# Layer 0 of a graph network: the record columns of the edges loaded turn by turn on SyncE

## What is computed

```python
edge_w = edge_attr @ nn_w.T + nn_b
msg = jax.nn.relu(x[src] * edge_w)
out = x @ root + bias
for r in range(N_REL):
    mask = edge_type == r
    m = jnp.where(mask[:, None], msg, 0.0)
    s = jax.ops.segment_sum(m, dst, num_segments=n)
    cnt = jax.ops.segment_sum(mask.astype(x.dtype), dst, num_segments=n)
    mean = s / jnp.maximum(cnt, 1.0)[:, None]
    out = out + mean @ W[r]
```

## Time and profile before

| | us |
|---|---|
| median of 3 runs | 6186.73 |
| lowest and highest run | 6183.74, 6193.87 |
| span of the profiled execution, first to last instruction | 4913.3 |
| edge stage of layer 0 in that span | 813.1 to 1386.7 |

### The profile page before, as it was taken

The page is one execution under the profiler, slowest core; times in us unless marked ns, Lnnn a source line. Parts: engine busy times, 40 slices in busy tenths (PEclk is TensorE's granted clock), DMA queues, the critical chain, the costliest instruction groups (busy, mean ns, idle before and its releaser), DMA issues. The chain is left out here.

```text
span 4913.3 us, 109595 instructions
## 1 busy us (share of the span) xinstructions
PE 3943.9 (80%) x22466; PEld 3257.1 (66%) x22467; DVE 3417.9 (70%) x9239; ACT 1796.7 (37%) x5526; POOL 3122.8 (64%) x3449
## 2 busy tenths in 40 slices
PE   6799995888987889878898466785978788478886
PEld 3577774777876677767777355674856666267664
DVE  7788885667757778577786667866247778755665
ACT  0455552221123333333332100002247667257774
POOL 0266664777756777667776677766677773057775
PEclk9999997999998999989999677997979889677877
DMA  1233334845516455164551687742456445134444
GB/s 45 92 125 128 125 126 102 212 126 157 161 49 190 137 150 156 55 192 136 150 157 31 208 255 217 247 125 65 148 166 133 106 106 127 43 99 108 109 109 100
DMA packets 651843, 647.50 MB, mean 132 GB/s; under 512 B 316126, under 2 KB 557860, under 8 KB 651716
## 3 DMA queue, kind: packets, MB, share of 16 engines
q0 software_dynamic: 145968, 374.55, 27.2%
q1 hardware_dynamic: 407764, 217.31, 16.2%
q10 hardware_dynamic: 97984, 54.35, 3.6%
HBM read 468.18 MB, written 176.82 MB: 131 GB/s over the span
## 5 line engine op out<-in xcount | busy, mean ns | idle before, releaser
L973 POOL DMA_INDIRECT G<-h_dram,idx x1572 | 1519.8, 967 | 537.1 <-issue 353.7
L1148 PEld LDWEIGHTS ps_a<-hotm,msg 128*128 128x128 f32 x4716 | 689.1, 194 | 199.3 <-DVE arena L1237 65.9
L1136 PE MATMUL ps_e<-nnw,attT 128*128 128x256 f32 x2358 | 736.3, 396 | 100.4 <-DVE prodm L1230 46.6
L1148 PE MATMUL ps_a<-hotm,msg 128*128 128x128 f32 x4716 | 730.6, 283 | 92.4 <-DVE arena L1237 91.6
L1237 DVE TENSOR_TENSOR arena<-ps_a,arena 128x256 f32 x1404 | 588.1, 419 | 215.6 <-issue 102.2
L768 POOL DMA_INDIRECT rec_dram<-rec,pos x392 | 376.4, 960 | 424.2 <-ACT rec L631 362.7
L973 POOL DMA_INDIRECT G<-feat_dram,idx x420 | 405.0, 964 | 350.9 <-POOLq L242 223.3
L1183 ACT ACTIVATE msg<-prodm 128x256 f32<-128x256 f32 x786 | 327.5, 417 | 670.9 <-DVE prodm L1230 602.5
L790 POOL DMA_INDIRECT rec_dram<-now,to x396 | 383.4, 968 | 186.3 <-POOL to L787 103.6
L1714 POOL DMA_INDIRECT arena<-rel_dram,idx x393 | 383.8, 977 | 123.9 <-issue 86.2
L1136 PEld LDWEIGHTS ps_e<-nnw,attT 128*128 128x128 f32 x2358 | 368.0, 196 | 137.8 <-DVE prodm L1230 67.3
(11 more groups left out here) (354 smaller groups left out, 7906.1 us busy)
## 6 DMA issues: line engine op xcount, KB each, us to landing
gate<-rec_dram SPq DMA_DIRECT2D x126, 384.0 KB
G<-msg_dram SPq DMA_DIRECT2D x300, 128.0 KB
msg_dram<-msg ACTq DMA_DIRECT2D x270, 128.0 KB
rel_dram<-stage SPq DMA_DIRECT2D x25, 1040.0 KB
G<-h_dram,idx POOLq DMA_INDIRECT x1572
msg_dram<-arena ACTq DMA_DIRECT2D x90, 128.0 KB
at<-edge_attr SPq DMA_DIRECT2D x98, 112.0 KB
attT<-attT_dram SPq DMA_DIRECT2D x74, 144.0 KB
```

The costliest lines, as they stand in the source:

```text
L973: pool.indirect_dma_start(G[:, n % width, :], None, table, bass.IndirectOffsetOnAxis(ap=idx[:, which, n:n + 1], axis=0)).then_inc(sem(f"sw ...
L1136: t.matmul(ps_e[s % BANKS][:], attT[:, s // HU, s % HU, :], nnw[:], start=True, stop=True).then_inc(sem("ew"), 1)
L1148: last = t.matmul(ps_a[s % BANKS][:, h, :], of[:, h * P:(h + 1) * P], hot[:, s, :], start=True, stop=True)
```

## The change

The columns of a turn now come in two turns ahead of their use (AHEAD0 = 2), all on SyncE. SyncE's first transfer has the columns of turn 0 alone (18 chunks), and then come six transfers of attributes. Once the first has landed, the columns of turns 1 and 2 follow (36 chunks), and only then the weights W, root and bias. After that each half turn brings three transfers of attributes of three chunks each (edge_rows; before, one of nine) and one transfer of columns for the turn after next (columns_in, nine chunks or fewer), which waits until the transfer of columns before it has landed. ScalarE issues no loads.

VectorE lays out the indices: those of turn 0 between two halves of the memset, those of turns 1 and 2 in turn 0 at step 9, and from turn 1 on, at step 9 of each turn, those of the turn after next. GpSimd casts nothing, and waits at each turn for its indices. TensorE waits for attributes every 3 units instead of every 9. VectorE's walk has one seam more (at turn 9), and its last two turns are written out instead of looped. Layers 1 and 2 keep the order of their work.

```diff
-        FIRST = 3 * U
+        AHEAD0 = 2
-        def columns_of(pool, first, end, loaded, loads):
...
-                        att = sb(pctx, "att", [P, 2, HU, A32]) if l == 0 else None
+                        att = sb(pctx, "att", [P, U, A32]) if l == 0 else None
...
-                                    sp.dma_start(meta[:, 0:FIRST, :], meta_rows[:, 0:FIRST, :]).then_inc(sem("meta_in0"), 16)
...
+                                def columns_in(turn, half, late):
+
+                                    sp.wait_ge(sem("meta_in"), (turn * 2 - 4 + half) * 16)
+                                    if late:
+                                        lo, hi = ((0, HU), (HU, FRONT))[half]
+                                        sp.dma_start(late_meta[:, ds(turn - SEAM), lo:hi, :].rearrange("p t s w -> p (t s) w"),
+                                                     rec_d[ds((turn * FRONT + SEAM * BACK + lo) * P, (hi - lo) * P), WMETA:WMETA + NMETA].rearrange(
+                                                         "(j p) w -> p j w", p=P)).then_inc(sem("meta_in"), 16)
+                                    else:
+                                        first = turn * U + half * HU
+                                        sp.dma_start(meta[:, ds(first, HU), :],
+                                                     rec_d[ds(first * P, HU * P), WMETA:WMETA + NMETA].rearrange(
+                                                         "(j p) w -> p j w", p=P)).then_inc(sem("meta_in"), 16)
+
+                                def edge_rows(i, h, after, late):
+
+                                    for q in range(h * (HU // QU), (h + 1) * (HU // QU)):
+                                        count = min(FRONT - q * QU, QU) if late else QU
+                                        if count <= 0:
+                                            continue
+                                        first = (i * FRONT + SEAM * BACK if late else i * U) + q * QU
+                                        sp.wait_ge(sem("attT"), upto(first + count - 1 - FRONT if after else first + QU - 1 - U))
+                                        sp.dma_start(att[:, q * QU:q * QU + count, :], rec_d[ds(first * P, count * P), WA32:REC].rearrange(
+                                            "(j p) w -> p j w", p=P)).then_inc(sem(f"att_in{q}"), 16)
...
+                                    sp.dma_start(meta[:, 0:U, :], meta_rows[:, 0:U, :]).then_inc(sem("meta_in"), 16)
+                                    for h in range(2):
+                                        edge_rows(0, h, False, False)
+                                    sp.wait_ge(sem("meta_in"), 16)
+                                    sp.dma_start(meta[:, U:3 * U, :], meta_rows[:, U:3 * U, :]).then_inc(sem("meta_in"), 16)
+                                    weights()
                                     extra_meta(0)
                                     halves = KD // BACK // 2
                                     with nc.sync.Fori(1, 1 + halves) as i:
                                         for h in range(2):
-                                            edge_columns(i, h, False, False)
+                                            edge_rows(i, h, False, False)
+                                            columns_in(i + AHEAD0, h, False)
                                             extra_meta(i * 2 - 1 + h)
...
+                                    with nc.sync.Fori(SEAM - AHEAD0, SEAM) as i:
+                                        for h in range(2):
+                                            edge_rows(i, h, False, False)
+                                            columns_in(i + AHEAD0, h, True)
...
+                                    with nc.sync.Fori(SEAM + 1, TURNS1 - AHEAD0) as i:
+                                        for h in range(2):
+                                            edge_rows(i, h, True, True)
+                                            columns_in(i + AHEAD0, h, True)
+                                        extras(i)
+                                    with nc.sync.Fori(TURNS1 - AHEAD0, TURNS1) as i:
+                                        for h in range(2):
+                                            edge_rows(i, h, True, True)
+                                        extras(i)
...
-                                    columns_of(pool, 0, FIRST, "meta_in0", 1)
-                                    gather_rows(pool, (0, FIRST - HU), h_d, 0, G, "prod", units=True)
-                                    columns_of(pool, FIRST, NU, "meta_in1", 1 + KD // BACK)
-                                    gather_rows(pool, (FIRST - HU, NU), h_d, 0, G, "prod", units=True)
+                                    for k in range(TURNS1):
+
+                                        pool.wait_ge(sem("columns"), k + 1)
+                                        gather_rows(pool, (k * U, (k + 1) * U), h_d, 0, G, "prod", units=True)
...
-                                        if s % HU == 0:
-                                            pe.wait_ge(sem(f"att_in{s // HU}"), (i + 1) * 16)
+                                        if s % QU == 0:
+                                            pe.wait_ge(sem(f"att_in{s // QU}"), (i + 1) * 16)
...
-                                if l == 0:
-                                    nc.scalar.dma_start(meta[:, FIRST:SEAM * U, :], meta_rows[:, FIRST:SEAM * U, :]).then_inc(sem("meta_in1"), 16)
-                                    for q in range(KD // BACK):
-                                        first = SEAM * U + q * FRONT
-                                        nc.scalar.dma_start(late_meta[:, q, 0:FRONT, :], meta_rows[:, first:first + FRONT, :]).then_inc(sem("meta_in1"), 16)
...
-                                v.memset(arena[:], 0.0).then_inc(sem("zeroed"), 1)
-                                dve.wait_ge(sem("zeroed"), 1)
+                                if l == 0:
+                                    half = KD * D // 2
+                                    v.memset(arena[:, 0:half], 0.0).then_inc(sem("zeroed"), 1)
+                                    dve.wait_ge(sem("meta_in"), 16)
+                                    v.tensor_copy(idx[:, 0, 0:U], meta[:, 0:U, 1]).then_inc(sem("columns"), 1)
+                                    v.memset(arena[:, half:KD * D], 0.0).then_inc(sem("zeroed"), 1)
+                                    dve.wait_ge(sem("zeroed"), 2)
...
+                                for c0, c2, c8 in walk(nc.vector, TURNS1, 0, 2, 8, seams=(KEPT, SEAM - AHEAD0, SEAM) if l == 0 else (SEAM,), late=True,
+                                                       static=AHEAD0 if l == 0 else 0):
+                                    if c0 and c0[2] == HU and l == 0:
+                                        n, i, s = c0
+                                        if isinstance(i, int) and i == 0:
+
+                                            dve.wait_ge(sem("meta_in"), 32)
+                                            v.tensor_copy(idx[:, 0, U:3 * U], meta[:, U:3 * U, 1]).then_inc(sem("columns"), 2)
+                                        elif not (isinstance(i, int) and i + AHEAD0 >= TURNS1):
+
+                                            dve.wait_ge(sem("meta_in"), (i + AHEAD0 - 1) * 32)
+                                            to = idx[:, 0, ds(n - HU + AHEAD0 * U, FRONT if c0.phase >= 2 else U)]
+                                            of = (late_meta[:, ds(i + AHEAD0 - SEAM), 0:FRONT, 1].rearrange("p t s -> p (t s)") if c0.phase >= 2
+                                                  else meta[:, ds(n - HU + AHEAD0 * U, U), 1])
+                                            v.tensor_copy(to, of).then_inc(sem("columns"), 1)
...
-                                        if l == 0:
-                                            dve.wait_ge(sem("columns"), i + 1)
```

More of the change, by code:

```diff
@@ L974, in gather_rows @@
                     ap=idx[:, which, n:n + 1], axis=0)).then_inc(sem(f"sw_g{n % width}"), 16)
-        FIRST = 3 * U
+        AHEAD0 = 2
         meta_rows = rec_d[0:NC1 * P, WMETA:WMETA + NMETA].rearrange("(j p) w -> p j w", p=P)
-        def columns_of(pool, first, end, loaded, loads):
-            pool.wait_ge(sem(loaded), 16 * loads)
-            if first == 0:
-                last = nc.gpsimd.tensor_copy(idx[:, 0, first:end], meta[:, first:end, 1])
-            else:
-                nc.gpsimd.tensor_copy(idx[:, 0, first:SEAM * U], meta[:, first:SEAM * U, 1])
-                last = nc.gpsimd.tensor_copy(idx[:, 0, SEAM * U:NU].rearrange("p (t s) -> p t s", s=U)[:, :, 0:FRONT],
-                                             late_meta[:, :, 0:FRONT, 1])
-            last.then_inc(sem("columns"), (end - first) // U)
-            pool.wait_ge(sem("columns"), end // U)
         def gathered_by(passes, s):
@@ L1063, in edge_columns @@
                                     before = first + count - 1 - FRONT if after else first + HU - 1 - U
-                                    if l == 0:
```

(27 more changed lines are left out.)

30 lines of the change are left out of this document (19 added, 11 removed).

## The result

The changed kernel is **slower**: a median of 6196.32 us (14 runs, 6186.22 to 6211.70) against 6184.12 us (14 runs, 6174.08 to 6194.97) of the kernel before, a ratio of 1.0022 with a 95% interval of 1.0012 to 1.0031. The forecast was 6170, some 17 us faster, with a range that ended at 6186.

A forecast was written before the change was run, and what follows sets the result against it. GpSimd was taken to pace layer 0's edge stage up to the seam, then a VectorE–TensorE chain. Terms -22.4 + 1.0 + 3.7 + 1.0 = -16.7 us gave 6170.0 from 6186.73, range 6160 to 6186.

The forecast's parts named there:

- the lead of 22.4 us: Layer 0's edge stage: earlier first gather, vanished idle time and pauses of GpSimd together, claimed as the gain at the seam.
- The first gather, -7.0 us: Start of layer 0: GpSimd's first gather at about 826.0 instead of 833.08, after VectorE's cast between the memset's halves.
- the idle 14.08 us, -13.8: Start of layer 0: GpSimd's wait for a first free slot shrinks to the usual 0.30 us.
- the first columns land no sooner: Rival: first columns of layer 0 land at 832 instead of 819.5; gain only 9.7 us, time 6177; chance 0.13.
- What the memset does to gathers: Start of layer 0: the memset's second half beside the first gathers costs them nothing.
- so a shift of GpSimd's start lasts to the seam: Layer 0: GpSimd paces up to the seam, so its earlier start, worth 22.4 us there, lasts to the end.
- no pause of GpSimd over 2 us up to the seam: Layer 0 before the seam: a sign in the trace that would show the forecast right.
- The casts, +1.0 and +3.7: VectorE's casts in layer 0: +1.0 us in early turns by delaying gathers, +3.7 in thirteen late turns at 0.28 each.
- TensorE +1.0: Late turns of layer 0: three more waits for attributes per turn, 0 to 2.2 us, taken as +1.0.
- SyncE's queue: Layer 0: SyncE's 6 attribute and 2 column loads per turn fit in its time; taken as 0.
- the slower rival: Layer 0: SyncE's queue gets late, columns land late and VectorE stands at step 9; up to 6216 us; chance 0.10.
- what fills that is untouched: The 1273.4 us between the profiled span of 4913.3 and the median 6186.73 were taken as unaffected by the change.

The follow-up runs named there:

- e9: As e1, but ScalarE's 16 column loads at the start are back and SyncE's later column loads are left out; ratio 1.0014 to the kernel before.
- e0: The kernel before, run once more unchanged for a trace to lay beside the changed kernel's; 6185.23 us, span 6183.0.
- e1: Changed kernel with 48 already met waits (24 instructions) ahead of VectorE's later loop, which then lies in three pieces; ratio 0.9979 to the kernel before.
- e10: Changed kernel with 96 already met waits (48 instructions) ahead of VectorE's later loop, which lies in three pieces; ratio 0.9990 to the kernel before.
- e11: Changed kernel with 256 already met waits (128 instructions) ahead of VectorE's later loop, which lies in four pieces; ratio 1.0067 to the kernel before.
- e2: Kernel before with 180 already met waits (90 instructions) ahead of VectorE's later loop, which then lies in four pieces; ratio 1.0053 to the kernel before.
- e5: As e1, with every later load of columns made twice on SyncE, the second into a buffer nothing reads; ratio 0.9986 to the kernel before.

## Why the prediction was wrong

Two steps failed. The sign was wrong because of a term that the sum does not have at all: what the longer program of VectorE does to a loop behind layer 0. And the sum lets the lead of 22.4 us pass through layer 0 with a loss of 5.7, where the traces show it shrinking to 13.8 at the seam and 4.0 at turn 25. Point by point:

- **The first gather, -7.0 us, and the idle 14.08 us, -13.8**: right at the start, not at the seam. The first columns had landed in time, the cast began 10.2 us into the stage (12.3 forecast) as the memset started earlier than in the first trace, the first message came at +21.7 (+22 forecast), and the lead at turn 1 was 22.1 us against a sum of -22.4. But the prediction has the 22.4 as the gain at the seam, and there it was 13.8. The rival "the first columns land no sooner" did not come.
- **What the memset does to gathers**: right, they take 0.95 us beside its second half.
- **"so a shift of GpSimd's start lasts to the seam, where GpSimd paces, and from there to the end"**: that the start reaches the end holds by e9 (15 to 21 us lost when it is undone), the reason does not. In the timed executions GpSimd does not set the pace: from turn 2 to turn 24 of e0 it stands waiting for free slots for 211.6 us, and where VectorE waits ahead of a message and the profile names no releaser, the gather of its rows had been issued 22 us or more before:

```profile
POOL G L973 <- DVE msg L1226: 211.6, 119, 9.9
```

The chain between TensorE, ScalarE and VectorE sets it. TensorE's waits in the first trace, 912 to 1364 us:

```profile
PE ps_a L1148 <- DVE arena L1237: 38.6, 36, 2.3
PE ps_e L1136 <- DVE msg L1226: 8.0, 11, 1.0
```

and in e0, turns 2 to 24 (1027 to 1650 us):

```profile
PE ps_e L1136 <- ACT attT L1169: 86.8, 51, 4.6
PE ps_a L1148 <- DVE arena L1237: 42.0, 34, 3.0
PE ps_a L1148 <- issue: 20.6, 15, 2.2
PE ps_e L1136 <- issue: 13.1, 14, 2.4
```

The waits for ScalarE and those for nothing visible are new. The sign that the prediction names, no pause of GpSimd over 2 us up to the seam, fails with them, in e0 as in the changed kernel.

- **The casts, +1.0 and +3.7, TensorE +1.0**: together too small for what layer 0 lost. The price of a cast was too low, but the runs do not show that casts make up the difference. The view of the cast's line in the changed kernel:

```profile
L1250 DVE CAST idx<-meta x23: 166/227/306, 987.4 to 1611.5; - x19, 128x13 int32<-128x13 f32 x3, 128x18 int32<-128x18 f32 x1
L1250 DVEq FUSED_REGOPS  x19: 93/105/123, 987.0 to 1611.3; - x19
L1250 DVEq ALU_OP  x12: 45/45/45, 1322.8 to 1611.4; - x12
```

A cast with its two register instructions is 0.38 us, not 0.28, which makes 4.9 in 13 turns. Gathers were not held up: in the changed kernel the 21 that ran beside one of these casts took 0.94 to 0.95 us, so the +1.0 of the early turns is not seen. With the loop in three pieces the change gains 13 us (e1, 0.9979; the 6 of e10 include some 7 of its own waits), where the sum had 16.7 and its bounds 10.5 to 22.4. But the stage itself, up to its last sum, is shorter by only 3.1 us in the changed kernel than in e0, and by 0.5, 5.5 and 1.6 in e1, e10 and e11 than in e2 (e10 and e11 on another chip). Where the rest of the 13 us lies, single profiles do not show.
- **SyncE's queue, and the slower rival**: it did not come. VectorE waits for no columns at step 9, and doubling the column loads (e5) changed nothing that can be told from no change. This rival forecast the right sign, at a chance of 0.10, but for a reason that the traces rule out; that it was slower is no credit to it.
- **"what fills that is untouched"**: wrong, as is the sentence ahead of the prediction that it rests on. The 1273.4 us were not outside of the span; the trace showed an execution that took a fifth less time than any timed one (4913.3 against 6183.0). A trace whose span doesn't fit the time by a fifth should have been a warning that its pace is not the timed one's.
- **The term that failed**: the sum has no line for what the change does to stages behind layer 0. It has no term for the new seam and the two written-out turns of VectorE, and gives no reason why they should be nothing. They and the casts are 373 instructions of code, and they moved a later loop over a boundary: some 27 us, which turned some 13 us gained (e1) into 12 lost (6196.32 against 6184.12).

## What to carry to other kernels

When a change makes an engine's program longer, look at every loop behind it on that engine: here a loop of 308 instructions cost some 27 us in eight passes when it came to lie in four pieces of 128 instead of three, and 24 instructions that do nothing gave them back. Keep such a filler short and look at its own time: 128 of them cost some 20 us. Compare the instruction queue's packets of the two traces first when a stage differs that the diff does not touch. And hold the span of a trace against the time of its runs before any row of it is used as a price.

## What was not expected of the hardware

The reload has two prices in the traces: 4.9 to 5.5 us at the loop's head per pass with the boundary near its head (changed kernel, e11), 3.6 to 3.9 where e2's boundary lay, against 1.1 without. Why some 40 of the waits of e2 and of e11, whose condition already holds, come 0.7 us or more behind the one before, when the others come 0.1 us apart or less, stays open.

The same program ran 26% longer in every timed run than in the first trace, and the clock explains only a part. In the first stage, 200 to 700 us, both have TensorE's granted clock at 1.00 (columns: busy us and instructions of PE, PEld, DVE, ACT and POOL, clock, DMA share, GB/s). First trace:

```profile
200.00:700.00 500.00, 500.00 (x3408) 396.81 (x3406) 435.00 (x1427) 267.87 (x713) 303.12 (x316) 1.00 0.39 126
```

e0:

```profile
200.00:700.00 500.00, 460.77 (x2924) 335.13 (x2924) 376.14 (x1226) 229.78 (x614) 264.38 (x273) 1.00 0.33 108
```

TensorE gets through 2924 instructions instead of 3408 in the same time. Single instructions on VectorE take as long in both (the one-hots 1.35 us); what is new in this stretch are stalls of 1 to 3 us with no visible cause, on VectorE, ScalarE and GpSimd. What makes them stays open.
